# Attention phase: a group's four normalisation tiles split between VectorE and GpSimd over two steps

## What is computed

```python
def _layernorm(x, axis=-1, eps=1e-05):
    m = jnp.mean(x, axis=axis, keepdims=True)
    v = jnp.var(x, axis=axis, keepdims=True)
    return (x - m) / jnp.sqrt(v + eps)
...
Q = (query @ Wq.T + bq).reshape(B, Nq, H, D).transpose(0, 2, 1, 3)
K = (key @ Wk.T + bk).reshape(B, Nkv, H, D).transpose(0, 2, 1, 3)
V = (value @ Wv.T + bv).reshape(B, Nkv, H, D).transpose(0, 2, 1, 3)
scores = jnp.einsum('bhqd,bhkd->bhqk', Q, K) * SCALE
scores = scores / temperature
attn = jax.nn.softmax(scores, axis=-1)
out = jnp.einsum('bhqk,bhkd->bhqd', attn, V)
out = out.transpose(0, 2, 1, 3).reshape(B, Nq, C)
return out @ Wo.T + bo
...
x = x + _L0_xattn_ref(_layernorm(x, axis=-1), ctx_1024, ctx_1024, ...)
```

## Time and profile before

| what | value |
|---|---|
| median of 3 executions | 1833.2 us (1832.55 to 1835.22) |
| the profiled execution: its own time | 1834.5 us |
| its span, first to last instruction | 1832.7 us |
| mean granted TensorE clock | 0.984 |
| TensorE matmul busy | 1757.0 us, 96% |
| VectorE busy | 1560.0 us, 85% |
| ScalarE busy | 1227.3 us, 67% |
| GpSimd busy | 969.5 us, 53% |

### The profile page before, as it was taken

How to read it: one execution, slowest core, us unless ns; L and a number is a source line. 1 busy time by engine, 2 the same in 40 slices (tenths; PEclk the granted TensorE clock), 3 DMA queues, 4 the chain that set the end, 5 groups by cost and what they waited for, 6 DMA issues and landing times. The chain is left out here.

```text
span 1832.7 us, 29920 instructions
## 1 busy us (share of the span) xinstructions
PE 1757.0 (96%) x9162; PEld 1303.6 (71%) x9162; DVE 1560.0 (85%) x3587; ACT 1227.3 (67%) x3374; POOL 969.5 (53%) x1076
## 2 busy tenths in 40 slices
PE   8897899999999999999879999889999999999997
PEld 7776688888888888888644444357767767777775
DVE  6766789999999999988669888878888988888885
ACT  4575899999999999999633333356556655665543
POOL 2334466666666666666510000147767767667665
PEclk9999999999999999999989999999999999999999
DMA  8666444555455445544379999155445445444311
GB/s 304 197 217 174 106 124 141 145 157 141 141 148 157 141 140 155 154 117 117 92 246 393 401 397 384 46 215 171 155 162 193 150 168 191 149 170 165 127 58 41
DMA packets 154478, 323.13 MB, mean 176 GB/s; under 512 B 47440, under 2 KB 55632, under 8 KB 136656
## 3 DMA queue, kind: packets, MB, share of 16 engines
q1 hardware_dynamic: 153840, 320.43, 53.5%
q10 hardware_dynamic: 480, 0.79, 0.2%
HBM read 164.90 MB, written 105.91 MB: 148 GB/s over the span
## 5 line engine op out<-in xcount | busy, mean ns | idle before, releaser
L1291 POOL TENSOR_TENSOR a_pr<-a_pr,a_rcp 128x512 f32<-128x512 f32 x256 | 266.7, 1042 | 268.9 <-DVE a_rcp L1135 268.4
L1043 ACT ACTIVATE a_pr<-a_s,a_nmax 128x128 f32<-128x128 f32 x1024 | 366.1, 386 | 25.9 <-DVE a_nmax L1128 23.9
L1043 ACT ACTIVATION_READ_ACCUMULATOR a_pr<-a_s,a_nmax 128x1 f32 x1024 | 229.1, 224 | 0.0
L1548 PE MATMUL f_pair<-f_room,w 128*128 128x512 bf16 x1024 | 228.0, 381 | 0.9 <-ACT f_room L1659 0.9
L1967 POOL TENSOR_TENSOR f_rs<-f_rs,f_half 128x1 f32<-128x1 f32 x128 | 121.3, 948 | 179.3 <-DVE f_rs L1814 179.3
L1768 DVE CUSTOM_DVE_ANT_0 f_hf<-f_pair,nb,sh 128x512 f32<-128x512 f32 x244 | 172.6, 748 | 28.1 <-PE f_pair L1548 27.9
L1697 ACT ACTIVATE f_room<-f_ring,f_off,f_rs 128x511 f32<-128x511 f32 (+1 forms) x128 | 104.3, 815 | 120.4 <-POOL f_off L1973 120.4
L1548 PEld LDWEIGHTS f_pair<-f_room,w 128*128 128x128 bf16 x1024 | 99.3, 98 | 116.1 <-issue 2.5
L1128 DVE TENSOR_REDUCE a_nmax<-a_s 128x4 f32<-128x512 f32 x256 | 171.7, 671 | 10.9 <-PE a_s L932 10.5
L1143 DVE TENSOR_TENSOR a_pTl<-a_pt,a_pTh 128x512 fp32r<-128x512 f32 x256 | 168.5, 679 | 12.5 <-ACT a_pTh L1055 12.4
L944 PE MATMUL a_pt<-ident,a_pr 128*128 128x128 f32 x1024 | 159.8, 279 | 19.7 <-POOL a_pr L1291 11.4
(11 more groups left out here) (393 smaller groups left out, 5000.6 us busy)
## 6 DMA issues: line engine op xcount, KB each, us to landing
hidden<-f_hf SPq DMA_DIRECT2D x57, 1024.0 KB, 8.5
f_hf<-hidden SPq DMA_DIRECT2D x57, 1024.0 KB, 4.8
xb<-x SPq DMA_DIRECT2D x16, 1024.0 KB, 5.4
a_xr<-x SPq DMA_DIRECT2D x64, 256.0 KB, 3.0
x<-a_xr SPq DMA_DIRECT2D x64, 256.0 KB, 2.2
f_ring<-x SPq DMA_DIRECT2D x64, 256.0 KB, 3.1
out<-f_ring SPq DMA_DIRECT2D x64, 256.0 KB, 2.6
ctxh<-bqreph SPq DMA_DIRECT2D x126, 128.0 KB, 2.4
```

What stands on the lines that cost most here:

```text
L1043: last = e.activation(pr[:, t, j, :], s_bank[t][:, j * P:j * P + P], ACT.Exp, bias=nmax[kk % 2][:, t, j:j + 1], accum_out=sums[kk % 2][:, ...
L1291: e.tensor_tensor(p, p, rcp[kk % 2][:, t, :].unsqueeze(2).to_broadcast([P, 4, KEYS]), ALU.mult).then_inc(*e_pn)
L1548: last = e.matmul(h_bank[(PAIRS * u + i) % 3][:, q, :], w1[:, k, f * P:f * P + P], xT[u % 2][:, k, :], start=k == 0, stop=k == KC - 1)
```

## The change

In phase 1 VectorE normalises tile 0 and GpSimd tile 1; in phase 2 VectorE normalises tile 2 and GpSimd tile 3. VectorE's place in the step is the old one; GpSimd's is between `prob` 0 and `prob` 1. VectorE's tiles raise `e_xn`, GpSimd's raise the new event `e_xn_odd`, and the first `xt` of a group waits for two of each. XT stays at 6, so that `xt` still comes in phase 2.

```diff
@@ -852,11 +852,12 @@
+        e_xn_odd = ev("xnodd")
...
-        LOAD, LN_A, LN_B, NORM, XT, QUERY = 11, 9, 8, 7, 6, 2
+        LOAD, LN_A, LN_B, NORM_A, NORM_B, XT, QUERY = 11, 9, 8, 7, 6, 6, 2
@@ -906,7 +907,8 @@
                 if k == 0:
-                    e_xn.wait_ge(e, b * GPB + g - NORMED)
+                    e_xn.wait_ge(e, 2 * (b * GPB + g - NORMED) + 1)
+                    e_xn_odd.wait_ge(e, 2 * (b * GPB + g - NORMED) + 1)
@@ -1223,18 +1225,16 @@
-            def norm(b, kk):
-                o = kk + NORM
+            def norm(b, kk, ahead, t):
+                o = kk + ahead
...
                 e_rs.wait_ge(e, G - NORMED)
-                for t in range(TPG):
-                    last = e.tensor_scalar(xb[g % 2][:, t, :], xb[g % 2][:, t, :], mv[g % 2][:, t, 0:1],
-                                           rs[g % 2][:, t:t + 1], ALU.subtract, ALU.mult)
-                last.then_inc(*e_xn)
+                e.tensor_scalar(xb[g % 2][:, t, :], xb[g % 2][:, t, :], mv[g % 2][:, t, 0:1],
+                                rs[g % 2][:, t:t + 1], ALU.subtract, ALU.mult).then_inc(*e_xn)
@@ -1258,7 +1258,8 @@
-                    norm(b, kk)
+                    norm(b, kk, NORM_A, 0)
+                    norm(b, kk, NORM_B, 2)
@@ -1319,6 +1320,17 @@
+            def norm(b, kk, ahead, t):
+                o = kk + ahead
+                if kk < 0 or o % 4 or not there(b, o):
+                    return
+                g, G = o // 4, b * GPB + o // 4
+                if isinstance(G, int) and G < NORMED:
+                    return
+                e_rs.wait_ge(e, G - NORMED)
+                e.tensor_scalar(xb[g % 2][:, t, :], xb[g % 2][:, t, :], mv[g % 2][:, t, 0:1],
+                                rs[g % 2][:, t:t + 1], ALU.subtract, ALU.mult).then_inc(*e_xn_odd)
@@ -1332,6 +1344,8 @@
                 prob(b, kk, 0)
+                norm(b, kk, NORM_A, 1)
+                norm(b, kk, NORM_B, 3)
                 prob(b, kk, 1)
```

## The result

The changed kernel takes 1844.99 us (median of 4 executions, 1842.36 to 1846.60) against 1833.64 us before (4 executions): ratio 1.0058, 95% interval 1.0046 to 1.0071. It is 11 us slower, where the forecast had 3.6 us faster. The profiled execution is the fastest of the four, 1842.36 us for a span of 1840.5 us.

What follows compares the result with a forecast made beforehand. TensorE, busy 96% of the span, was taken as the bound, so only its waits count: 11 x 0.32 = 3.5 us plus 0.1 at the first sets, 1833.2 - 3.6 = 1829.6 us, range 1828.0 to 1834.5.

Steps and rivals of the forecast that it cites:

- d: Length of GpSimd's normalisation of one tile in phases 1 and 2: taken as 1.0 us, with ends 0.7 and 1.3.
- the estimate of 0.8: GpSimd's tile by the Trainium skill's page: nearer to 0.8 us, the product starting 0.2 us sooner, the sum the same.
- the date of `pt`: TensorE wants `pt` at step start + 6.20 us; GpSimd's product costs nothing up to about + 6.15.
- the excess past it: TensorE's loss in a step: past about + 6.23 us each nanosecond is paid, excess = product end - 6.23.
- 28 steps against 14: Slower case: late products in 28 steps of phases 1 and 2, against 14 phase-1 steps before.
- The slower rival: GpSimd's tile goes first, VectorE's ends 0.3 us after it and delays the reciprocal: + 4.0 us, 1837.2; chance 0.14.
- simply over 1.5 us long: Added to the slower case: a GpSimd tile of over 1.5 us gives the same end; within its chance of 0.14.
- The gain to be had: TensorE's phase-1 waits for GpSimd's product vanish, 11 x 0.32 = 3.5 us, plus 0.1 from the first sets: 3.6 us.
- the excess of phase 1: The phase-1 step with four normalisations lasts 0.32 us over TensorE's own 11.25 us.
- the 0.70 us of waiting for ScalarE: VectorE's idle time in phase 2 before the reciprocal, said to cover its added tile at no cost.
- the hold on GpSimd by VectorE: Where the two normalisations meet, VectorE goes first and holds up GpSimd's tile by at most 0.28 us.
- VectorE's busy time: Over the kernel, said to fall by 28 x 0.5 = 15 us.

Runs made afterwards that it cites:

- e6: The changed kernel with GpSimd normalising only 384 columns of tiles 1 and 3, nobody the last 128: 1833.95 us against 1833.62 before.
- e8: The changed kernel run again without an edit, beside more executions of the kernel before: 1844.84 us against 1833.62.
- e1: Against the changed kernel, VectorE normalises two tiles in each of phases 1 and 2, GpSimd none: 1831.27 us against 1833.07 before.
- e7: Against the changed kernel, GpSimd does only tile 1, behind `xbo` in phase 1; VectorE tile 0, then 2 and 3 in phase 2: 1828.54 us against 1833.62 before.
- e10: The kernel of e7 again, side by side with that of e1: 1830.11 us against 1833.21 before.

## Why the prediction was wrong

- **The step that failed is the price of GpSimd's tile.** The prediction bounded d from above by the 1.28 us of an addition with two streams, since "one stream should not cost more". It costs more: 2.09 us alone, 2.25 in place, against the 1.0 forecast and the 1.3 of its upper end; the estimate of 0.8 beside it lay further off still. The nearest row I took, the broadcast multiplication at 1.04 us, was near in what it reads but is another instruction. The rows of before did hold a tensor_scalar on GpSimd, at 128x1 only, and its 0.27 us says nothing of the price of a column.
- **With the right d the forecast's own sum gives the sign.** It had the date of `pt`, the excess past it, and 28 steps against 14. From d = 2.25 the product would end at 3.64 + 2.25 + 1.04 = +6.93; measured +6.92. The formula's excess, 0.70 us, was too high by 0.15, as TensorE makes up part of it (e6). So its sum would be 28 x 0.70 - 3.6 = 16 us slower, and with the measured 0.55 us it is 11.8; 11.4 was measured.
- **The slower rival named the wrong mechanism first.** VectorE's tile was not held behind GpSimd's: it took 0.63 us, as in the earlier trace rows, and the reciprocal came at +4.12 in phase 1 and +4.20 in phase 2, waiting for ScalarE only, as forecast. Where GpSimd did begin first (e8, at 235 us), VectorE's tile ended 1.05 us before GpSimd's and not 0.3 us after it. The half-sentence on a tile "simply over 1.5 us long" was the case that happened, though by the prediction's own formula the gain is used up only at d = 1.68, and 0.2% slower comes at 1.81. The chance of 0.14 was too low for a price that no row showed.
- **The gain to be had was forecast about right.** e1 and e7 remove the excess of phase 1 without GpSimd in the way and give 1.8 to 5.1 us, 3.2 with both side by side, for the 3.6 forecast. VectorE's tiles in phase 2 are covered by the 0.70 us of waiting for ScalarE.
- **Wrong in size:** the hold on GpSimd by VectorE, 0.16 us and not 0.28. VectorE's busy time fell by 8.5 us and not by 15: a tile in a row of four added only about 0.46 us, and a tile by itself takes 0.63. The Trainium skill ("SBUF — State Buffer", Who interferes with whom) states that where the two want the shared pair of ports, whoever asks first has it for its whole instruction and the other is blocked. The records here don't show a hold of that length: a VectorE tile of 256 columns and one of 512 cost GpSimd 0.16 us each, less than their records of 0.40 and 0.64 us, and behind GpSimd's 2.09 us VectorE lost 0.3. The trace doesn't show which of the two was reading or writing when, so what part of a record holds the ports stays open.
- ScalarE's waits for the DMAs of the query planes, mostly at changes of sequence as in the step of the earlier trace rows, differ between executions of one kernel: from 243 to 800 us 0.7 us in all in e7's profile and 3.4 in e10's, of the same kernel. Before has 4.4 us of them in its profile, the changed kernel 0.6, and the steps that they lengthen make up to 3 us of difference between two profiles. That is most of why the profiled span of the changed kernel is only 7.8 us over that of before.

## What to carry to other kernels

Before an operation is moved to another engine, its price there at its full width has to be known; an operation that reads less is not a bound from above for one that reads more on GpSimd. Here a multiplication with a second input took 1.04 us, an addition 1.28, and a tensor_scalar with one tile as input and two operations 2.09. Look where the receiving engine waits, not only how much: the same 2.1 us cost 0.55 us a step in front of a product with a date and nothing behind `xbo`. And when an engine is late once in four steps, splitting its own work over two steps can be enough.

## What the runs showed of the hardware

On GpSimd, 128x512 in f32: a copy 0.61 us, a multiplication by a broadcast column 1.04, an addition of two tiles 1.28, a tensor_scalar with one operation 1.50 to 1.57, with two operations 1.93 to 2.09. A VectorE tensor_scalar that begins before GpSimd's and runs into it lengthens GpSimd's by 0.16 us; one that began 0.2 us after it left GpSimd's at 2.09 us and took 0.83 us itself instead of 0.54.
